# Attention with relative positions and mixture-of-experts block: lo stores begun from GpSimd's queue, maxima and loads in another order

## The reference

```python
q, k, v = split(x @ qkv_w + qkv_b)          # 12 heads, hd = 32, S = 2304 tokens
attn  = (q * hd**-0.5) @ k.T
rel_h = einsum('bhwc,hkc->bhwk', q, Rh)     # for each token, a value per key row    (48)
rel_w = einsum('bhwc,wkc->bhwk', q, Rw)     # for each token, a value per key column (48)
attn  = softmax(attn + rel_h[..., :, None] + rel_w[..., None, :])
out   = (attn @ v) @ proj_w + proj_b
```

## Time and profile before

| what | value |
|---|---|
| median of 3 runs | 2257.36 us (2256.86 to 2262.19) |
| the profiled execution's own time | 2257.31 us |
| its span | 2255.6 us |
| mean granted TensorE clock | 0.94 of full speed |
| busy share of PE, DVE, ACT, POOL | 93%, 79%, 73%, 33% |

### The profile page before, as it was taken

The page is one execution under the profiler, slowest core; times in us unless marked ns, Lnnn a source line. Parts: engine busy times, 40 slices in busy tenths (PEclk is TensorE's granted clock), DMA queues, the critical chain, the costliest instruction groups (busy, mean ns, idle before and its releaser), DMA issues. The chain is left out here.

```text
span 2255.6 us, 38092 instructions
## 1 busy us (share of the span) xinstructions
PE 2097.3 (93%) x12644; PEld 1938.3 (86%) x12644; DVE 1781.2 (79%) x3334; ACT 1650.2 (73%) x2908; POOL 754.0 (33%) x519
## 2 busy tenths in 40 slices
PE   6958889999999999999999999685999999999997
PEld 6957778888888888888888888463999999999997
DVE  5647879999998999899999997376777777777774
ACT  3344468888888888888888889512777877777885
POOL 0060034454445444544454445421112122111211
PEclk9955599999999999999999999886999999999998
DMA  6889783565446455564565444223666767767674
GB/s 212 253 232 269 246 146 67 110 110 105 88 86 131 87 106 90 105 120 75 110 110 103 94 82 99 86 86 110 200 223 207 224 213 219 226 210 222 209 221 106
DMA packets 121594, 338.20 MB, mean 150 GB/s; under 512 B 17984, under 2 KB 57496, under 8 KB 114740
## 3 DMA queue, kind: packets, MB, share of 16 engines
q1 hardware_dynamic: 109152, 308.88, 53.1%
q0 software_dynamic: 10400, 19.87, 4.1%
q10 hardware_dynamic: 1920, 7.88, 1.5%
HBM read 269.62 MB, written 66.97 MB: 149 GB/s over the span
## 5 line engine op out<-in xcount | busy, mean ns | idle before, releaser
L972 DVE TENSOR_REDUCE mx<-ps_m 128x1 f32<-128x384 f32 x1212 | 642.3, 552 | 111.4 <-PE ps_m L847 105.6
L721 POOL TENSOR_TENSOR p_lo<-p_f,p_hi 128x768 fp32r<-128x768 f32 x216 | 405.9, 1879 | 710.4 <-ACT p_f L934 710.4
L928 ACT ACTIVATE p_hi<-ps_s 128x768 fp32r<-128x768 f32 x648 | 528.1, 815 | 156.3 <-PE ps_s L861 152.7
L934 ACT ACTIVATE p_f<-ps_s 128x768 f32<-128x768 f32 x648 | 525.4, 811 | 1.3 <-POOL p_lo L721 1.3
L721 DVE TENSOR_TENSOR p_lo<-p_f,p_hi 128x768 fp32r<-128x768 f32 x432 | 425.0, 984 | 33.2 <-ACT p_f L934 32.4
L847 PE MATMUL ps_m<-all_keys,query_hi 128*128 128x384 f32 x1212 | 411.5, 344 | 19.5 <-DVE mx L972 10.3
L1642 ACT CAST w_hi<-w_raw 128x384 fp32r<-128x384 f32 x600 | 290.1, 516 | 136.0 <-PE ps_o L1619 127.3
L1760 DVE TENSOR_TENSOR w_lo<-w_raw,w_hi 128x384 fp32r<-128x384 f32 x600 | 316.5, 556 | 78.5 <-ACT w_hi L1642 78.4
L858 PE MATMUL ps_s<-query_hi,all_keys 128*128 128x384 f32 x1296 | 336.8, 341 | 6.4 <-SPq L782 5.7
L871 PE MATMUL ps_o<-p_hi,val 128*65 128x384 f32 x1296 | 331.7, 337 | 1.9 <-POOL p_lo L721 1.7
L871 PE MATMUL ps_o<-p_lo,val 128*65 128x384 f32 x1296 | 332.6, 338 | 0.0
(11 more groups left out here) (199 smaller groups left out, 2991.9 us busy)
## 6 DMA issues: line engine op xcount, KB each, us to landing
w_raw<-w_u SPq DMA_DIRECT2D x200, 576.0 KB, 5.0
query_rest<-rel_lo_d SPq DMA_DIRECT2D x36, 864.0 KB
query_rest<-q_hi_d SPq DMA_DIRECT2D x36, 576.0 KB
query_rest<-q_lo_d SPq DMA_DIRECT2D x36, 576.0 KB
rel_hi_d<-room SPq DMA_DIRECT2D x6, 2016.0 KB, 13.3
rel_lo_d<-out_lo SPq DMA_DIRECT2D x6, 2016.0 KB, 18.3
query_hi<-rel_hi_d SPq DMA_DIRECT2D x24, 432.0 KB, 18.6
v_d<-v_sb SPq DMA_DIRECT2D x6, 1170.0 KB, 8.0
```

The costliest lines, as they stand in the source:

```text
L721: engine.tensor_tensor(p_lo[r][:], p_f[idx % 2], p_hi[r][:].bitcast(F32), ALU.subtract).then_inc(lo_done(0, idx)[0], 1)
L928: act.activation(p_hi[r][:], ps_s[:, bank:bank + 2, 0:TB], ACT.Exp).then_inc(hi_ok, 1)
L934: act.activation(p_f[idx % 2], ps_s[:, bank:bank + 2, 0:TB], ACT.Exp).then_inc(f_ok, 1)
L972: dve.tensor_reduce(mx[s // TILES][:, s // 3 % 6, col:col + 1], ps_m[:, c, 0:TB], AX.X, ALU.max).then_inc(mx_ok, 1)
```

## The change

Two things of `phase_rel` change, and one of `phase_attention`:

- The lo part of each group is stored from GpSimd's DMA queue (`store_low`) and counted on semaphores of its own (`low_out`). GpSimd issues the store of group 0 between its two calls of `one_hots`, those of groups 1 to 5 after the second. SP stores only the hi part and waits for no lo part any longer, save before the load of `query_rest`. ACT waits for the hi stores alone, DVE for the lo stores alone.
- The first chunk comes after fill 60 (`FIRST_FILL` 2 * 24 + 12) instead of fill 48, and the 30 spread chunks share 84 fills instead of 96. The load of `query_rest` for the first block moves from behind group 0's store to behind group 3's.
- At the start of `phase_attention` SP issues `query_rest` of block 1, the row of maxima, `load_hi` for the second head, and only then `query_rest` of block 2; `load_hi` no longer waits for the first scores.

```diff
@@ -440,8 +440,9 @@
         ROWS = (slice(0, UP), slice(UP, UP + SIDE))
         BOTH = UP + SIDE
         CHUNKS = UNITS - SHIFT
-        FIRST_FILL = 2 * FILLS
+        FIRST_FILL = 2 * FILLS + FILLS // 2
         BEHIND = 12
+        REST_GROUP = 3
         chunk_after = {}
         for s in range(CHUNKS - BEHIND):
             chunk_after.setdefault(FIRST_FILL + s * (ALL - FIRST_FILL) // (CHUNKS - BEHIND), []).append(s)
@@ -462,6 +463,7 @@
         r_hi = sem("r_hi")
         r_lo = sem("r_lo")
         r_out = [sem(f"r_out{i}") for i in range(2)]
+        low_out = [sem(f"low_out{i}") for i in range(2)]
         hi_in = sem("hi_in2")
         rest_in = sem("rest_in2")
         mm_ok = sem("mm_ok2")
@@ -480,10 +482,8 @@
 
             def store(g):
                 sp.wait_ge(r_hi, FILLS * (g + 1))
-                sp.wait_ge(r_lo, FILLS * (g + 1))
-                for o, d in ((out_hi, rel_hi_d), (out_lo, rel_lo_d)):
-                    sp.dma_start(d[g * RH:(g + 1) * RH, 0:BOTH, :].rearrange("h r n -> r h n"),
-                                 o[g % 2][0:BOTH, :, :].bitcast(F32)).then_inc(r_out[g % 2], 16)
+                sp.dma_start(rel_hi_d[g * RH:(g + 1) * RH, 0:BOTH, :].rearrange("h r n -> r h n"),
+                             out_hi[g % 2][0:BOTH, :, :].bitcast(F32)).then_inc(r_out[g % 2], 16)
 
             def store_max(b):
                 sp.wait_ge(negt_ok, b + 1)
@@ -496,8 +496,10 @@
                     load_keys(sp, 0, keys[0], k_hi_d, hi_in)
                     sp.wait_ge(hot_ok, HOT_STEPS)
                     load_rest_keys(sp, 0, keys[1], k_hi_d, k_lo_d, val, v_d, rest_in)
-                    sp.wait_ge(r_out[0], 32)
+                    sp.wait_ge(r_out[0], 16)
                     load_query(sp, 0, query_hi, q_hi_d, rel_hi_d, hi_in)
+                if g == REST_GROUP:
+                    sp.wait_ge(low_out[0], 16)
                     load_query_rest(sp, 0, 0, query_rest, q_hi_d, q_lo_d, rel_lo_d, rest_in)
                 if g == GROUPS - 1:
                     store_max(0)
@@ -506,13 +508,22 @@
                     sp.dma_start(query_rest[TOP - 1:TOP, :, :].bitcast(F32),
                                  m_d[0:1, 0:QB].rearrange("r (a n) -> r a n", a=1).broadcast_to([1, VARIANTS, QB])).then_inc(rest_in, 16)
             for i in range(2):
-                sp.wait_ge(r_out[i], 32 * GROUPS // 2)
+                sp.wait_ge(r_out[i], 16 * GROUPS // 2)
+                sp.wait_ge(low_out[i], 16 * GROUPS // 2)
             sp.wait_ge(rest_in, 16 * 8)
 
         @block.gpsimd
         def _(pool):
+            def store_low(g):
+                pool.wait_ge(r_lo, FILLS * (g + 1))
+                pool.dma_start(rel_lo_d[g * RH:(g + 1) * RH, 0:BOTH, :].rearrange("h r n -> r h n"),
+                               out_lo[g % 2][0:BOTH, :, :].bitcast(F32)).then_inc(low_out[g % 2], 16)
+
             made = one_hots(pool, keys[0], keys[1], hot[:], hot_ok)
+            store_low(0)
             one_hots(pool, keys[2], keys[3], hot[:], hot_ok, made)
+            for g in range(1, GROUPS):
+                store_low(g)
 
         @block.tensor
         def _(pe):
@@ -579,7 +590,7 @@
             for n in range(ALL):
                 g = n // FILLS
                 if n % FILLS == 0 and g >= 2:
-                    act.wait_ge(r_out[g % 2], 32 * (g // 2))
+                    act.wait_ge(r_out[g % 2], 16 * (g // 2))
                 act.wait_ge(ps_ok, n + 1)
                 if n == turn_fill:
                     act.copy(neg_mt[0][:], ps[0:6, n % BANKS, TB:TB + P]).then_inc(negt_ok, 1)
@@ -602,7 +613,7 @@
             for n in range(ALL):
                 g = n // FILLS
                 if n % FILLS == 0 and g >= 2:
-                    dve.wait_ge(r_out[g % 2], 32 * (g // 2))
+                    dve.wait_ge(low_out[g % 2], 16 * (g // 2))
                 dve.wait_ge(r_hi, n + 1)
                 dve.tensor_tensor(places(out_lo, n), results(n), places(out_hi, n).bitcast(F32), ALU.subtract).then_inc(r_lo, 1)
                 for s in chunk_after.get(n, ()):
@@ -782,10 +793,11 @@
             sp.sem_inc(rest_in[0], REST_LOADS)
             sp.sem_inc(negt_ok, 2)
             sp.sem_inc(m_out, 16)
-            for b in range(1, QBLOCKS):
-                load_query_rest(sp, 0, b, query_rest[b], q_hi_d, q_lo_d, rel_lo_d, rest_in[b])
+            load_query_rest(sp, 0, 1, query_rest[1], q_hi_d, q_lo_d, rel_lo_d, rest_in[1])
             load_max(0, 1)
-            start(0, 0)
+            load_hi(1, 1)
+            load_query_rest(sp, 0, 2, query_rest[2], q_hi_d, q_lo_d, rel_lo_d, rest_in[2])
+            load_max(0, 2)
             for h in range(HEADS - 1):
                 rest(h, h % 2)
 
```

## The result

The changed kernel takes 2235.27 us (median of 4 runs, 2232.83 to 2240.33), the kernel before 2258.49 (4 runs, 2256.86 to 2262.19). The ratio is 0.9898, with a 95% interval of 0.9876 to 0.9919, that is 23 us less (18 to 28). The prediction was 2234.7, with 2222 to 2246 as its range. The profiled execution took 2235.09 us, its span is 2233.3 us, 22.3 less than before.

The account below looks back on a forecast made before the run. TensorE's two waits for the hi query, set by bytes loaded ahead of it, held the whole effect; 7.5 + 2 + 0 + 1 + 12.1 = 22.6 us off 2257.3 gave 2234.7 us, range 2222 to 2246.

Parts of the forecast that it names:

- The waits and their sizes: TensorE's two long waits for the hi query: 24.0 us in the relative-position stage, 9.2 us in the first attention head.
- The signs that I had named for being right: Chunk 0 wait 11 to 13 us, last hi store 249 to 252, no unit 12 wait, attention clock 1.0 from 285 us.
- Step a: Relative-position stage: later first chunk hides 11 more fills in the wait for the hi query, gaining 7.5 us.
- Step b: Relative-position stage: `query_rest` behind group 3 lets group 1's stores land before fill 72, giving back 2 of 3.2 us.
- Step c: Relative-position stage: lo stores on GpSimd's queue land about 15 us after issue, within a 20 us group; effect 0.
- Step d: Stage's end: less stands ahead of the maxima's small write in SP's queue; at most 2 us, taken as 1.
- Step e: Attention start: fewer bytes ahead of the hi query remove the 9.2 us wait and half clock behind it; 12.1 us.
- The hi query didn't land sooner (1): Relative-position stage: loads overlap lo stores, chunk 0 comes at 172, another 7 us gained, 2223 to 2228; chance 0.15.
- for the lo store (2): Only one of the stage's and attention's waits goes: 2245 or 2240 us; chance 0.16.
- Rival 3: Relative-position stage: GpSimd-queue lo stores outlast a group, cancelling the gain from 25.7 us landing, 2275 at 30; chance 0.06.

Follow-up runs that it names:

- run 1: Kernel before with only the new order of loads at the start of the attention stage: 2247.12 us, ratio 0.9948.
- run 2: Changed kernel with the old order of loads at the start of the attention stage: 2243.55 us, ratio 0.9942.
- run 3: Changed kernel with lo stores issued from SP again, each behind its hi store, on their own semaphore: 2232.83 us, ratio 0.9896.
- run 6: Kernel before with only the first chunk moved later (`FIRST_FILL = 2 * FILLS + FILLS // 2`): 2259.64 us, ratio 1.0030.
- run 7: Kernel before with only the load of `query_rest` moved behind group 3's stores: 2252.94 us, ratio 0.9991.
- run 5: Kernel before with only lo stores on GpSimd's queue and their separate semaphores and waits: 2249.68 us, ratio 0.9979.
- run 9: Kernel before with lo stores on GpSimd's queue, separate waits and the later first chunk; `query_rest` early, attention as before: 2256.71 us, ratio 0.9997.
- run 4: Changed kernel with lo keys, second hi keys and v loaded behind group 3 instead of ahead of the hi query: 2228.00 us, ratio 0.9876.
- run 8: Changed kernel with lo keys, second hi keys and v loaded behind group 1, not ahead of the hi query: 2224.82 us, ratio 0.9871.
- run 10: As run 8, with the two writes of the maxima issued from ACT's queue instead of SP's: 2225.34 us, ratio 0.9857.
- 11: As run 8, with the first chunk behind fill 72 (`FIRST_FILL = 3 * FILLS`): 2235.72 us, ratio 0.9905.
- 12: As run 10, with the first chunk behind fill 72 (`FIRST_FILL = 3 * FILLS`): 2234.88 us, ratio 0.9906.

## Why the prediction was right, point by point

**The waits and their sizes.** The stages of both waits hold the whole effect, and within the intervals runs 1 and 2 show their gains to be independent. The price of loads at 208 GB/s gave the landing of the hi query: 179 forecast, 178.26 in run 3, and 181.20 in the changed kernel, of which 1.2 is the later start of the stage. Counted from the stage's start it ends the wait 53.9 to 56.4 us later in all nine kernels with the same bytes ahead of it, and 47.6 to 50.4 us later in the three with 1161 KB fewer. The signs that I had named for being right were met in part: the last hi store (251.33), no wait at unit 12 and the full clock, yes; a wait of 11 to 13 us before chunk 0, no: it is 6.2, since 9.4 went into the wait for the lo store.

**Step a, the later first chunk (7.5).** The sum of a and b (9.5) was near what the trace shows (8.8), the split wrong. Alone the later chunk loses 5 to 7 us (run 6). It only moves fills ahead of the wait; what they win is kept only if fill 72 finds its buffers free, and with `query_rest` ahead of group 1's stores it doesn't. The step also miscounts by one: chunk 0 stands behind fill 60, not 59, so 12 fills move and not 11, worth 6.6 us by DVE's price and 9.0 by TensorE's. And 7.5 was a choice between two prices, so that the sum came out within 1 us, and the time within 1 us of the forecast where the interval is 10 us wide, is in part luck.

**Step b, `query_rest` behind group 3 (2).** Alone 2 us, the number that I gave, but not clear of none (run 7), and its trace has new waits in place of the one that went. Such waits I had put at 0. It is the condition of a, which the step didn't see: I priced ACT's 3.2 us wait as it stood and not as it becomes when the fills come 12 sooner (17.1 us in run 6). Together with the separate waits, and with the lo stores on SP, they give the stage's whole gain: run 3 against run 1 is 0.0052, 11.7 us with some 6 either way, where a and b were 9.5. What the separate waits add to that no run shows; the prediction has no term for them.

**Step c, the queue (0).** In the final combination it is 0 (run 3). With `query_rest` in front of the stores, queue and separate waits together are worth more: 4.7 us in run 5, and 0.0033, 7.5 us with some 4 either way, from run 6 to run 9 (the stages of their traces differ by 1.7 us only). What was wrong in the step is the landing: both at about 158 was said, the hi store was used at 156.6, the lo store landed at 167.7, 23.6 us after its issue instead of 15. That is over the 20 us of a group, and that it cost nothing is luck: the step's 0 rested on the 20 us, and the cover was the hi query's wait. The rule of the Trainium skill ("SBUF — State Buffer", the two separate sides) that GpSimd's DMAs starve while VectorE runs a 2-port operation isn't put to the test: DVE's operations in this stretch are the subtractions, which read PSUM (`ps`) beside `room`. Nor does a busy DVE explain the late landing: from 144 to 158 us it is busy 11.5 us in the changed kernel and 11.0 in run 4, where the store takes 14.6 us, and for the last 10.7 us before the landing it stands idle. Runs with keys and v ahead of the hi query have 23.6, 19.2 (run 2), 18.8 (5) and 18.5 (9), those without 14.6 (4), 15.4 (8), 15.9 (10), 15.0 (11) and 15.3 (12). What differs is the loads that share the DMA engines; how they hold the store back wasn't taken apart, and the change and run 2 have the same stage, so 4 us between two executions is scatter.

**Step d, the end of the stage (1).** 1.4 in the trace. The wait for the maxima's write is 4.4 to 4.6 us in the four kernels with the old stores (before, runs 1, 6 and 7) and 2.8 to 3.0 in the changed one and runs 2, 3, 5, 8, 9 and 11. But the mechanism was wrong: it isn't that less stands ahead in SP's queue, for in run 3 both stores still do, and SP waits 2.8 us. What run 3 shares with the changed kernel is that the last hi store no longer waits for the lo part and starts sooner, measured by DVE's last subtraction; that this is the cause is my reading and no run has it alone. Run 4, with more loads under way, waits 7.3 us.

**Step e, attention (12.1).** 12.2 in the trace, 11.7 by run 1's ratio, 10.4 by run 1's trace. The hi query's bytes ahead, counted, gave the landing (about 291 us, 23 us after the stage's first load, as forecast), and the clock stayed up. How much of the 12 is the half clock wasn't tried by itself; 9.2 of them were the wait. The 2 us between the two traces go with the clock at the stage's start: at half for 3.5 us after the first matmul in the changed kernel, for 7.6 us in run 1. The row of maxima behind block 2's `query_rest` now waits 5.3 us (299.35 to 304.92 in SP's queue), and TensorE has no wait for it.

**The rivals.** The hi query didn't land sooner (1); the wait at unit 12 went, and of the 24.0 us in the stage 6.2 are left behind the 9.4 for the lo store (2). Rival 3 named the right place, and came nearer than 0.06 suggests: 23.6 us for group 0's store, of the four on which a later group waits, and covered; those of groups 1 to 3 took 17.4 to 20.3 us, and nothing waited 2 us for them.

## What to carry to other kernels

When a first use waits for a transfer, add up the bytes queued ahead of it, divide by the rate that this kind of transfer shows in the trace, and reorder by first use: that gave both landings here within 2 us of the forecast, counted from the stage's start, and then a better kernel (run 8, keys and v out of the way: 2224.8 us). Work that is pulled forward into a wait is won only if the next thing it needs is also there sooner; look for the next release (here the buffers at fill 72) before you count it. Two edits that a sum prices apart (-7.5 and -2) may be one: alone they were +6.8 and -2 (not clear of none), together, with the separate waits, -11.7. And before you compare two kernels from one event to another, ask whether that event waits for the same things in both: the last hi store here does not, and counted from it the gain at the stage's end would come out as nothing.

## What the runs showed of the hardware that wasn't expected

- Group 0's store of 2016 KB on GpSimd's queue lands 14.6 to 15.9 us after its issue without the loads of keys and v ahead of the hi query, 18.5 to 23.6 with them; the last group's, beside a hi store alone, 13.6 (the changed kernel). GpSimd itself is held for 0.65 to 0.93 us by each.
- SP waits 2.8 us for a write of 3 KB with an unfinished store of 2016 KB ahead of it in the same queue (run 3, where the write lands 2.0 us before that store), and 3.0 us with that store in another queue. A queue of its own gained nothing (run 10).
- TensorE's clock stayed at half through the whole relative-position stage in every kernel, with the wait of 24 us and without it; in attention it went back to full within 10 us of the start (3.5 in the changed kernel, 7.6 in run 1) and, in the first head, fell again only behind the wait of 7.5 to 9.7 us for the hi query. In the relative-position stage TensorE was busy all the time in long stretches too, as from 184 to 200 us in the changed kernel (16.0 of 16 us, clock 0.50).
